# A float32 product replaced by three float32r passes in a one-core local-attention stack

## The chip, the cores and the metric

One core of one Trainium2 chip runs the whole kernel as a single program. The metric is device time in microseconds (us). TensorE (PE) multiplies; VectorE (DVE), ScalarE (ACT) and GpSimd (POOL) work on vectors; SyncE (SP) issues the DMAs.

## The reference, cut to what matters

Tokens: 1 x 2048 x 128, float32. A six-layer stack runs twice, with the same weights, and between the two runs stands a linear-attention block with a feed-forward part of its own. Each layer of the stack is:

```
x = attn_layer(shift_tokens(x)) + x     # 16 heads of 64, windows of 32 tokens, l2-normed q and k
x = ffn_layer(shift_tokens(x)) + x
def ffn_layer(x, g, bln, W1, b1, W2, b2):
    xn = (x - mu) / sqrt(var + 1e-05) * g + bln
    hg = xn @ W1 + b1                   # W1: 128 x 682
    a, gate = split(hg, 2)              # 341 each
    return a * gelu(gate) @ W2 + b2
```

The change is in `xn @ W1` and in the buffer that holds `a * gelu(gate)`.

## The kernel before, in words

**Tiling.** Activations lie transposed, 128 features on the partitions. The attention works on chunks of 128 tokens, 16 a layer (`CH`), the feed-forward on groups of 512 tokens, 4 a layer (`NG`). `stack(inv)` is written once for each engine and called twice. It is a software pipeline: each engine runs a loop over `t` (about 108 steps), and in step `t` does its share of chunk `t`, `t - 1`, `t - 2` and so on. Step `t` of PE overlaps step `t` of ACT and of DVE and step `t + 1` of POOL.

**The feed-forward in four phases.** `phase(n)` gives `(n - LAG) % 4` and the group. In phase 0 PE centres the group (L528) and makes the variances (L560); in phase 1 POOL makes the diagonals (L1290), PE spreads them (L531), DVE multiplies (L1029, `XN`), ACT adds the bias in place (L811, `xn_done`). In phases 2 and 3 PE makes the wide layer: `hidden` (L513 to L519) multiplies 114, 114 and 113 columns of `W1` with `XN` (128 x 512), float32; phase 2 makes the gate (ACT's gelu into `GB`, L815), phase 3 the other half (DVE's product into `HT`, L1036). In phase 1 of the next group PE multiplies `HT` with `W2` (L545, `y_done`). One product of each phase stands in `ffn_first`, ahead of the transposes of keys and queries (L340, `turn_keys`, `turn_queries`); two stand at the end of PE's step (`ffn_second`, `ffn_third`), ahead of the next step's scores (L450, L439). 48 groups, 2 phases, 3 products: 288 products. A float32 product is two records in the profile.

**The attention's projection.** `project` (L388 to L390) already multiplies in three passes, of a high and a low part each of the activation (`XH`, `XL`) and of the weights (`WH`, `WL`), all float32r. The weights' parts are made one layer ahead, in thirds `k` = 0, 1, 2: SP loads a third into `WSTAGE` (L1387), ACT rounds it in phase 1 (L804), POOL subtracts in phase 2 (L1299, `w_split`). Third 0 is split in phase 2 of the last group of the layer before, third 1 in that of the layer's first group, third 2 in that of its second.

**GpSimd's step**, in order: sines of the queries (L1240), low part of `x` (L1217, L1220), `add_keys` (L1282), `add_queries` (L1266), `ffn` (L1290 in phase 1, L1299 in phase 2), `scale_queries` (L1275, waits for the norms that DVE makes at L918), the table (L1234), sines of the keys (L1240, wait for PE's transposes). `turn_queries` on PE waits for L1275.

**SyncE's step** (L1376 to L1399) for chunk `c`: `window_values` waits for ACT's copy of the values (L770, `v_kept`) and issues 16 DMAs (L1373, L1374); then a rotary table (L1336). In steps 1, 5 and 9 of a layer it waits for `w_split` (L1386) before it loads the next third, in step 7 for the products of the layer before (`hid`) before it loads `W1`, in step 9 for `y_done` before it loads `W2`. ACT's copy L770 of chunk `c` waits for the window DMAs of chunk `c - 1` (L767), and PE's projection of the next keys (L388) waits for L770.

Of the kernel before, what the change touches and what calls it, by code (L numbers as in the profile page):

```python
# [7 lines left out]
F32 = mybir.dt.float32  # L8
F32R = mybir.dt.float32r
BF16 = mybir.dt.bfloat16  # L10
I32 = mybir.dt.int32
ALU = mybir.AluOpType
ACT = mybir.ActivationFunctionType
AX = mybir.AxisListType

P = 128
NTOK = 2048
CH = 16
GT = 512
NG = NTOK // GT  # L20
DEPTH = 6
HEADS = 16
# [4 lines left out]
DI = 341  # L27
# [10 lines left out]
NGR = DEPTH * NG  # L38

S_G, S_B, S_B2, S_B1A, S_B1G, NSMALL = 0, 1, 2, 3, 6, 9  # L40
# [54 lines left out]
def build(nc, a, out):  # L95
    ctx = ExitStack()
    with ctx:  # L97
        def sb(name, shape, dt=F32):
            return ctx.enter_context(nc.sbuf_tensor(name, shape, dt))

        def sem(name):
            return ctx.enter_context(nc.semaphore(name))
# [19 lines left out]
        WO = sb("WO", [P, 2, NP_, P])  # L122
        QKS = sb("QKS", [P, 2, 4 * DH])
        W1 = sb("W1", [P, 2 * DI])
        W2 = sb("W2", [P, 3, P])
        SMALL = sb("SMALL", [P, 2, NSMALL])

# [1 line left out]
        XL = sb("XL", [P, 2, P], F32R)  # L129
        RAWQK = sb("RAWQK", [P, 2, HEADS, DH])  # L130
        SQ = sb("SQ", [P, 2, HEADS, DH])
        SSM = sb("SSM", [P, HEADS])
        RN = sb("RN", [P, 2, HEADS + 4])
        NY = sb("NY", [P, NORMS])
        NV = sb("NV", [P, NORMS])
# [3 lines left out]
        QT = sb("QT", [P, NP_, P])  # L139
        KT = sb("KT", [P, NP_, WIN + P])  # L140
        MX = sb("MX", [P, 2, NP_])
        SUM = sb("SUM", [P, 2, HEADS])
        PR = sb("PR", [P, HEADS, 2 * WIN])
        PT = sb("PT", [P, NP_, P])
# [7 lines left out]
        DIAG = D2  # L152
        DG = sb("DG", [P, GT])
        XN = sb("XN", [P, GT])
        GB = sb("GB", [P, 3, GT])
        HT = sb("HT", [P, 3, GT])

        def flat(x):
            return x.rearrange("p a b c -> p (a b c)")
# [27 lines left out]
        PS = ctx.enter_context(nc.psum_tensor("PS", [P, 8, 512], F32))  # L187
# [19 lines left out]
        weighed = [sem("weighed%d" % r) for r in range(2)]; o_scaled = sem("o_scaled"); o_rows = sem("o_rows"); o_kept = sem("o_kept")  # L207
        projected = sem("projected"); xb_done = sem("xb_done"); xa_done = sem("xa_done")
        xf_done = sem("xf_done"); centred = sem("centred"); d2_done = sem("d2_done"); dg_done = sem("dg_done"); var_done = sem("var_done"); var_kept = sem("var_kept")
        diag_done = sem("diag_done"); spread = sem("spread"); z_done = sem("z_done"); xn_done = sem("xn_done")  # L210
        hid = [sem("hid%d" % i) for i in range(3)]; gelu_done = sem("gelu_done"); ht_done = sem("ht_done"); y_done = sem("y_done")
        m_cen = sem("m_cen"); m_d2 = sem("m_d2"); m_dg = sem("m_dg"); m_var = sem("m_var"); m_r = sem("m_r")
        m_diag = sem("m_diag"); m_rb = sem("m_rb"); m_ln = sem("m_ln")
# [9 lines left out]
        A_DMAS, F1_DMAS, F2_DMAS, V2_DMAS = 3, 1, 2, 16  # L223
# [22 lines left out]
        def group_count(inv, g):  # L246

            return inv * NGR + g + 1
# [39 lines left out]
        def _(pe):  # L288
# [55 lines left out]
            def stack(inv):  # L344
# [168 lines left out]
                def hidden(g, t, bank):  # L513
                    at, n = FT[t % 3]
                    at += 0 if t >= 3 else DI
                    if g % NG == 0:
                        pe.wait_ge(f1_w, 16 * F1_DMAS * (inv * DEPTH + g // NG + 1))
                    pe.wait_ge(xn_done, group_count(inv, g))
                    pe.matmul(PS[0:n, bank, :], W1[:, at:at + n], XN[:, :], start=True, stop=True).then_inc(hid[t % 3], 1)  # L519

                def ffn_first(n):
                    q, g = phase(n)
# [14 lines left out]
                def ffn_second(n):  # L537
                    q, g = phase(n)
                    if q == 1 and 0 <= g - 1 < NGR:
# [4 lines left out]
                        for i, (_, m) in enumerate(FT):  # L544
                            mm = pe.matmul(PS[:, B_F2, :], W2[0:m, i, :], HT[0:m, i, :], start=(i == 0), stop=(i == 2))  # L545
                        mm.then_inc(y_done, 1)
# [75 lines left out]
            for g in range(NG):  # L622
                q = group(QB, g)
# [17 lines left out]
            for g in range(NG):  # L641
                for n in range(4):
                    if g > 0:
                        pe.wait_ge(mg_ready, 4 * g - 3 + n)
                    pe.matmul(PS[:, 3 + n, :], FC1[:, n * P:(n + 1) * P], XNM[:, g, :], start=True,
                              stop=True).then_inc(mh_ready, 1)
# [15 lines left out]
        def _(act):  # L662
# [12 lines left out]
            def stack(inv):  # L675
# [116 lines left out]
                def ffn_late(n):  # L792
                    q, g = phase(n)
                    if q == 3 and 0 <= g + 1 < NGR:
                        act.wait_ge(xb_done, count(inv, 4 * (g + 1) + 3))
                        at = (g + 1) % NG * GT
                        held(centred, group_count(inv, g))
                        act.activation(XF[0:DH, :], XB[0:DH, at + 1:at + 1 + GT], ACT.Copy)
                        act.activation(XF[DH:P, :], XB[DH:P, at:at + GT], ACT.Copy).then_inc(xf_done, 1)
                    if q == 1 and 0 <= n < NCH and n % CH >= 4:  # L800
                        k, w = (n % CH) // 4 - 1, layer_of(inv, n) + 1
                        if w < 2 * DEPTH:
                            act.wait_ge(w_in, 16 * (3 * w + k - 2))
                            act.activation(WH[:, w % 2, k * HEADS * DH:(k + 1) * HEADS * DH], WIN_[:, :],  # L804
                                           ACT.Copy).then_inc(w_high, 1)
                    if not 0 <= g < NGR:
                        return
                    s = (inv * DEPTH + g // NG) % 2
                    if q == 1:
                        act.wait_ge(z_done, group_count(inv, g))  # L810
                        act.activation(XN[:, :], XN[:, :], ACT.Identity, bias=SMALL[:, s, S_B:S_B + 1]).then_inc(xn_done, 1)  # L811
                    elif q == 2:
                        for i, (_, m) in enumerate(FT):
                            act.wait_ge(hid[i], 2 * (inv * NGR + g) + 1)
                            act.activation(GB[0:m, i, :], PS[0:m, (B_F1, B_F2, B_F3)[i], :], ACT.Gelu,  # L815
                                           bias=SMALL[0:m, s, S_B1G + i:S_B1G + i + 1]).then_inc(gelu_done, 1)

# [36 lines left out]
            for g in range(NG):  # L854
                a = 2 * (g % 2)
# [10 lines left out]
            for g in range(NG):  # L866
                for n in range(4):
                    act.wait_ge(mh_ready, 4 * g + n + 1)
                    if g >= 2:
                        act.wait_ge(my_ready, g - 1)  # L870
                    act.activation(HTM[g % 2][:, n, :], PS[:, 3 + n, :], ACT.Gelu,
                                   bias=MSMALL[:, M_FC1B + n:M_FC1B + n + 1]).then_inc(mg_ready, 1)
# [10 lines left out]
        def _(dve):  # L883
# [37 lines left out]
            def stack(inv):  # L921
# [54 lines left out]
                def row_max(c):  # L976
# [4 lines left out]
                    s = rows(B_S).rearrange("p b (j k) -> p b j k", k=2 * WIN)  # L981
                    dve.tensor_reduce(MX[:, :, :], s, AX.X, ALU.max)  # L982
                    dve.drain()
# [69 lines left out]
            def norm_all(b, o, bias=None, done=None, at=(5, 6)):  # L1053
                dve.wait_ge(m_var, 4 * b + 4)
                dve.tensor_copy(SSM[:, :], PS[:, VAR, 0:16])
                dve.drain()
                r = RN[:, 0, 0:HEADS]
                rsqrt([(r, slice(0, HEADS))], SSM[:, :], NY[:, 0:HEADS], NU[:, 0:HEADS], NV[:, 0:HEADS], EPS, ALU.add).then_inc(m_r, 1)
                dve.drain()
# [24 lines left out]
            def norm_twice(b, first, second, gain, bias):  # L1084
                dve.wait_ge(m_var, 4 * b + 4)
                dve.tensor_copy(SSM[:, :], PS[:, VAR, 0:16])
                dve.tensor_copy(SUM[:, 0, :], PS[:, VAR, 0:16])
                dve.drain()
                r, rr = RN[:, 0, 0:HEADS], RN[:, 1, 0:HEADS]
                rsqrt([(r, slice(0, HEADS))], SSM[:, :], NY[:, 0:HEADS], NU[:, 0:HEADS], NV[:, 0:HEADS], EPS, ALU.add).then_inc(m_r, 1)  # L1090
                dve.drain()
                dve.scalar_tensor_tensor(SSM[:, :], SUM[:, 0, :], RSQRT_UNIT * RSQRT_UNIT, r, ALU.mult, ALU.mult)
                dve.drain()
                dve.tensor_tensor(SSM[:, :], SSM[:, :], r, ALU.mult)
                dve.drain()
# [100 lines left out]
        def _(pool):  # L1196
            def held(signal, value):

                if value > 0:
                    pool.wait_ge(signal, value)  # L1200
# [8 lines left out]
            def stack(inv):  # L1209
# [74 lines left out]
                def ffn(n):  # L1284
                    q, g = phase(n)
                    if q == 1 and 0 <= g < NGR:
                        c = n - 1 + CHAIN_OFF
                        pool.wait_ge(norms, chain_count(inv, c))
                        for j in range(4):
                            ins = pool.tensor_scalar(DIAG[:, j * P:(j + 1) * P], EYE[:, :],  # L1290
                                                     RN[:, c % 2, HEADS + j:HEADS + j + 1], None, ALU.mult)
                        ins.then_inc(diag_done, 1)
                    m = n - 1
                    if q == 2 and 0 <= m < NCH and m % CH >= 4:
                        k, w = (m % CH) // 4 - 1, layer_of(inv, m) + 1
                        if w < 2 * DEPTH:
                            pool.wait_ge(w_high, 3 * w + k + 1)
                            cols = slice(k * HEADS * DH, (k + 1) * HEADS * DH)
                            pool.tensor_tensor(WL[:, w % 2, cols], WIN_[:, :], WH[:, w % 2, cols].bitcast(F32),  # L1299
                                               ALU.subtract).then_inc(w_split, 1)  # L1300
# [16 lines left out]
        def _(sp):  # L1317
# [26 lines left out]
            def load_w1(w):  # L1344
                l = w % DEPTH
                sp.dma_start(W1[:, :], a["w1"][l:l + 1].rearrange("l p n -> p (l n)")).then_inc(f1_w, 16)

            def load_w2(w):
                l = w % DEPTH
                sp.dma_start(W2[0:FT[0][1], 0:2, :],  # L1350
                             a["w2"][l:l + 1, 0:FT[2][0]].rearrange("l (i p) n -> p (l i) n", i=2)).then_inc(f2_w, 16)
                sp.dma_start(W2[0:FT[2][1], 2, :], a["w2"][l:l + 1, FT[2][0]:DI].rearrange("l p n -> p (l n)")).then_inc(f2_w, 16)

# [109 lines left out]
```

## Time and profile before

| | us |
|---|---|
| median of 3 runs | 3620.34 (3605.24 to 3626.68) |
| the profiled execution, its own time | 3621.26 |
| its span, first to last instruction | 3619.1 |
| PE busy | 3322.5 (92%) |
| DVE busy | 2800.4 (77%) |
| POOL busy | 2720.1 (75%) |
| ACT busy | 2482.6 (69%) |
| mean granted TensorE clock | 0.969 of 2.4 GHz |

The two stacks take nearly all of the span, from about 35 to 1756 us and from about 1910 us to the end. Matmuls overlap in the array, so the distance from the start of one matmul to the start of the next says what it costs PE, and the length of its record does not.

### The profile page before, as it was taken

The numbers are of one execution on the slowest core, as the hardware profiler recorded it, in microseconds if no ns is written. First come the engines' busy times: TensorE is split into PE (matmuls) and PEld (weight loads), VectorE is DVE, ScalarE is ACT, GpSimd is POOL, SyncE is SP. The second block draws the span as 40 slices with busy tenths as digits, with TensorE's granted clock in tenths as the row PEclk, the third lists the DMA queues.
The fourth block names the chain that finished last, engine by engine and source line by source line (L and its number), as shares of the span: only waits on it lengthen the run. The fifth ranks groups of instructions, "written<-read, shape, count | busy, mean of one in ns | idle before, by whom it ended". The sixth has DMA issues, their size and how long they took to land. (4 is left out here: it accounts for less than half of the span.)

```text
span 3619.1 us, 152088 instructions
## 1 busy us (share of the span) xinstructions
PE 3322.5 (92%) x64040; PEld 2535.6 (70%) x64040; DVE 2800.4 (77%) x4983; ACT 2482.6 (69%) x3080; POOL 2720.1 (75%) x2152
## 2 busy tenths in 40 slices
PE   6899999999999999998677899999999999999996
PEld 4777777777777777776335777777777777777774
DVE  5778878788878878876447788778888878878883
ACT  4677777777767777775225677777777777777773
POOL 5888888788878878875007888888888888888881
PEclk8999999999999999999889999999999999999998
DMA  3333333333333333332002333333333333333320
GB/s 96 77 83 82 80 83 82 78 86 79 79 84 78 80 87 77 81 88 64 6 0 67 79 85 82 80 84 78 83 86 78 81 83 80 81 83 77 78 74 25
DMA packets 208997, 272.66 MB, mean 75 GB/s; under 512 B 55748, under 2 KB 103744, under 8 KB 208320
## 3 DMA queue, kind: packets, MB, share of 16 engines
q1 hardware_dynamic: 208320, 262.94, 28.2%
q8 instruction: 510, 8.36, 1.0%
q14 instruction: 167, 1.37, 0.1%
HBM read 60.35 MB, written 1.05 MB: 17 GB/s over the span
## 5 line engine op out<-in xcount | busy, mean ns | idle before, releaser
L1240 POOL TENSOR_TENSOR V<-RAWQK,TAB 128x512 f32<-128x512 f32 x768 | 953.2, 1275 | 443.5 <-PE PS L340 434.3
L388 PE MATMUL PS<-WH,XH 128*128 128x512 f32 x1152 | 518.4, 450 | 99.9 <-ACT VS L770 86.3
L770 ACT ACTIVATE VS<-PS 128x1024 f32<-128x1024 f32 x192 | 196.5, 1023 | 481.0 <-PE PS L390 357.2
L1282 POOL TENSOR_TENSOR V<-V,U 128x1024 f32<-128x1024 f32 x192 | 455.6, 2373 | 14.9
L390 PE MATMUL PS<-WL,XH 128*128 128x512 f32 x1152 | 465.5, 404 | 0.0
L389 PE MATMUL PS<-WH,XL 128*128 128x512 f32 x1152 | 464.5, 403 | 0.0
L1266 POOL TENSOR_TENSOR V<-V,U 128x1024 f32<-128x1024 f32 x192 | 457.5, 2383 | 0.0
L1275 POOL TENSOR_TENSOR V<-V,RN 128x1024 f32<-128x1024 f32 x192 | 372.2, 1938 | 93.7 <-DVE RN L918 92.1
L340 PEld LDWEIGHTS PS<-EYE,V 128*128 128x128 f32 x3072 | 348.2, 141 | 110.2 <-issue 99.0
L510 PEld LDWEIGHTS PS<-OT,WO 128*128 128x128 f32 x3072 | 373.6, 192 | 21.4 <-issue 5.1
L340 PE MATMUL PS<-EYE,V 128*128 128x128 f32 x3072 | 371.3, 274 | 10.3 <-ACT OT L777 5.1
L510 PE MATMUL PS<-OT,WO 128*128 128x128 f32 x3072 | 375.8, 276 | 3.3 <-DVE XN L1029 3.1
L439 PEld LDWEIGHTS PS<-KT,QT 64*32 64x32 f32 x24576 | 263.1, 105 | 126.4 <-issue 125.2
L940 DVE TENSOR_TENSOR U<-PS,TAB 128x1024 f32<-128x1024 f32 x192 | 234.3, 1220 | 139.9 <-issue 110.0
L439 PE MATMUL PS<-KT,QT 64*32 64x64 f32 x24576 | 303.0, 225 | 37.7 <-issue 37.1
L474 PE MATMUL PS<-V,PT 64*32 64x64 f32 x24576 | 336.4, 224 | 0.8 <-issue 0.4
L388 PEld LDWEIGHTS PS<-WH,XH 128*128 128x128 f32 x1152 | 223.5, 194 | 154.3 <-issue 98.0
L982 DVE TENSOR_REDUCE MX<-PS 128x16 f32<-128x1024 f32 x192 | 234.3, 1220 | 113.0 <-PE PS L439 112.0
L474 PEld LDWEIGHTS PS<-V,PT 64*32 64x32 f32 x24576 | 273.0, 105 | 68.1 <-issue 64.5
L519 PE MATMUL PS<-XN,W 128*114 128x512 f32 (+1 forms) x576 | 297.9, 630 | 5.3 <-ACT XN L811 4.6
L1002 DVE TENSOR_TENSOR ON<-PS,SUM 128x1024 f32<-128x1024 f32 x192 | 235.1, 1225 | 82.7 <-PE PS L474 75.3
L699 ACT ACTIVATE RAWQK<-PS 128x1024 f32<-128x1024 f32 x192 | 196.7, 1025 | 117.2 <-PE PS L390 117.2
(162 smaller groups left out, 7100.0 us busy)
## 6 DMA issues: line engine op xcount, KB each, us to landing
V<-VS SPq DMA_DIRECT2D x3072, 64.0 KB
ROTB<-c_rot SPq DMA_DIRECT2D x192, 128.0 KB, 2.5
WSTAGE<-wqkv SPq DMA_DIRECT2D x33, 512.0 KB
WO<-wo SPq DMA_DIRECT2D x12, 512.0 KB, 3.8
W<-w SPq DMA_DIRECT2D x12, 341.0 KB, 3.1
QKS<-qks SPq DMA_DIRECT2D x12, 128.0 KB, 3.7
W<-w SPq DMA_DIRECT2D x12, 114.0 KB
RAWQK<-x SPq DMA_DIRECT2D x4, 256.0 KB, 3.7
```

The costliest lines, as they stand in the source:

```text
L340: mm = pe.matmul(PS[:, bank + h // 4, (h % 4) * P:(h % 4 + 1) * P], src(h), EYE[:, :], is_transpose=True, start=True, stop=True, skip_grou ...
L388: pe.matmul(o, XH[:, p, :], WH[:, w, cols], start=True, stop=False)
L389: pe.matmul(o, XL[:, p, :], WH[:, w, cols], start=False, stop=False)
L390: mm = pe.matmul(o, XH[:, p, :], WL[:, w, cols], start=False, stop=True)
L439: mm = pe.matmul(PS[WIN * w:WIN * (w + 1), B_S + r, j * 2 * WIN:(j + 1) * 2 * WIN], QT[DH * r:DH * (r + 1), j, WIN * w:WIN * (w + 1)], KT[ ...
L474: mm = pe.matmul(PS[WIN * w:WIN * (w + 1), B_O + r, j * DH:(j + 1) * DH], PT[DH * r:DH * (r + 1), j, WIN * w:WIN * (w + 1)], V2[DH * r:DH ...
L510: mm = pe.matmul(PS[:, B_WO, 0:P], WO[:, w % 2, h, :], OT[:, h, :], start=(h == 0), stop=(h == NP_ - 1))
L519: pe.matmul(PS[0:n, bank, :], W1[:, at:at + n], XN[:, :], start=True, stop=True).then_inc(hid[t % 3], 1)
L1240: ins = pool.tensor_tensor(paired(V[:, k])[:, :, :, h * half:(h + 1) * half], split(RAWQK[:, k])[:, :, :, (1 - h) * half:(2 - h) * half], ...
L1266: pool.tensor_tensor(V[:, 0], V[:, 0], U[:, 0], ALU.add).then_inc(q_turned, 1)
L1275: pool.tensor_tensor(v, v, rn, ALU.mult).then_inc(q_scaled, 1)
L1282: pool.tensor_tensor(V[:, 1], V[:, 1], U[:, 1], ALU.add).then_inc(k_turned, 1)
```

## The change

`W1` is split once a layer, and `XN` once a group, into float32r high and low parts; `hidden` makes three passes. ACT writes `XNH` before it writes `XN`, and rounds `W1` after it when the group is its layer's first. POOL makes `W1L` (in the first group) and `XNL` in its phase-2 slot, ahead of L1299. PE waits for `xn_low` and `w1_low`. `HT` becomes another name of `GB`, and the gelu waits for the product with `W2` of the group before. `SSM` becomes another name of `MX`.

```diff
+        W1H = sb("W1H", [P, 2 * DI], F32R)
+        W1L = sb("W1L", [P, 2 * DI], F32R)
...
-        SSM = sb("SSM", [P, HEADS])
...
+        SSM = MX[:, :, :].rearrange("p a b -> p (a b)")
...
+        XNH = sb("XNH", [P, GT], F32R)
+        XNL = sb("XNL", [P, GT], F32R)
         GB = sb("GB", [P, 3, GT])
-        HT = sb("HT", [P, 3, GT])
+        HT = GB
...
                     if g % NG == 0:
-                        pe.wait_ge(f1_w, 16 * F1_DMAS * (inv * DEPTH + g // NG + 1))
-                    pe.wait_ge(xn_done, group_count(inv, g))
-                    pe.matmul(PS[0:n, bank, :], W1[:, at:at + n], XN[:, :], start=True, stop=True).then_inc(hid[t % 3], 1)
+                        pe.wait_ge(w1_low, inv * DEPTH + g // NG + 1)
+                    pe.wait_ge(xn_low, group_count(inv, g))
+                    pe.matmul(PS[0:n, bank, :], W1H[:, at:at + n], XNH[:, :], start=True, stop=False)
+                    pe.matmul(PS[0:n, bank, :], W1H[:, at:at + n], XNL[:, :], start=False, stop=False)
+                    pe.matmul(PS[0:n, bank, :], W1L[:, at:at + n], XNH[:, :], start=False, stop=True).then_inc(hid[t % 3], 1)
...
                         act.wait_ge(z_done, group_count(inv, g))
+                        act.activation(XNH[:, :], XN[:, :], ACT.Identity, bias=SMALL[:, s, S_B:S_B + 1])
                         act.activation(XN[:, :], XN[:, :], ACT.Identity, bias=SMALL[:, s, S_B:S_B + 1]).then_inc(xn_done, 1)
+                        if g % NG == 0:
+                            act.wait_ge(f1_w, 16 * F1_DMAS * (inv * DEPTH + g // NG + 1))
+                            act.activation(W1H[:, :], W1[:, :], ACT.Copy).then_inc(w1_high, 1)
                     elif q == 2:
                         for i, (_, m) in enumerate(FT):
                             act.wait_ge(hid[i], 2 * (inv * NGR + g) + 1)
+                            held(y_done, group_count(inv, g - 1))
...
+                    if q == 2 and 0 <= g < NGR:
+                        if g % NG == 0:
+                            pool.wait_ge(w1_high, inv * DEPTH + g // NG + 1)
+                            pool.tensor_tensor(W1L[:, :], W1[:, :], W1H[:, :].bitcast(F32), ALU.subtract).then_inc(w1_low, 1)
+                        pool.wait_ge(xn_done, group_count(inv, g))
+                        pool.tensor_tensor(XNL[:, :], XN[:, :], XNH[:, :].bitcast(F32), ALU.subtract).then_inc(xn_low, 1)
                     m = n - 1
                     if q == 2 and 0 <= m < NCH and m % CH >= 4:
                         k, w = (m % CH) // 4 - 1, layer_of(inv, m) + 1
```

## Rows read from the trace of the kernel before

**Rows 1.** The page: busy us, share of the span, instructions.

```profile
PE 3322.5 (92%) x64040; PEld 2535.6 (70%) x64040; DVE 2800.4 (77%) x4983; ACT 2482.6 (69%) x3080; POOL 2720.1 (75%) x2152
```

**Rows 2.** Window: length, busy of PE, PEld, DVE, ACT, POOL; PEclk, DMA, GB/s.

```profile
789.00:960.00 171.00, 167.56 (x3428) 130.72 (x3434) 145.78 (x252) 129.75 (x161) 141.47 (x114) 1.00 0.32 82
```

**Rows 3.** Waits: engine, line, releaser; us in total, times, longest.

```profile
SPq L1387 <- POOL WL L1299: 197.1, 22, 10.2
...
ACT VS L770 <- issue: 123.8, 25, 8.8
...
PE PS L388 <- ACT VS L770: 86.3, 30, 5.6
```

**Rows 4.** Timelines of POOL, SP, ACT, PE around the second stall of a layer.

```profile
739.61 4.97 POOL L1240 TENSOR_TENSOR V<-RAWQK,TAB 128x512 f32<-128x512 f32 x4 [2.09 <-PE PS L340]
...
765.85 2.40 POOL L1299 TENSOR_TENSOR WL<-WSTAGE,WH 128x1024 fp32r<-128x1024 f32 x1
...
768.27 0.33 SPq L1387 DMA_DIRECT2D WSTAGE<-wqkv  x1
...
784.03 1.02 ACT L770 ACTIVATE VS<-PS 128x1024 f32<-128x1024 f32 x1 [5.69 <-issue]
...
785.20 0.77 PE L388 MATMUL PS<-WH,XH 128*128 128x512 f32 x1 [4.17 <-ACT VS L770]
```

**Rows 5.** The same around the first stall of that layer.

```profile
693.27 2.39 POOL L1299 TENSOR_TENSOR WL<-WSTAGE,WH 128x1024 fp32r<-128x1024 f32 x1
...
710.82 1.02 ACT L770 ACTIVATE VS<-PS 128x1024 f32<-128x1024 f32 x1 [4.84 <-issue]
...
711.99 0.47 PE L388 MATMUL PS<-WH,XH 128*128 128x512 f32 x1 [3.54 <-ACT VS L770]
```

**Rows 6.** PE's timeline: six float32r matmuls, then one and two float32 products.

```profile
604.71 0.50 PE L388 MATMUL PS<-WH,XH 128*128 128x512 f32 x1
605.05 0.40 PE L389 MATMUL PS<-WH,XL 128*128 128x512 f32 x1
...
606.21 1.95 PE L510 MATMUL PS<-OT,WO 128*128 128x128 f32 x16
...
630.62 1.11 PE L519 MATMUL PS<-XN,W 128*114 128x512 f32 x2
631.57 1.91 PE L340 MATMUL PS<-EYE,V 128*128 128x128 f32 x16
...
634.20 1.97 PE L519 MATMUL PS<-XN,W 128*114 128x512 f32 x4
636.00 0.59 PE L450 MATMUL PS<-MASK,EYEB 128*128 128x512 bf16 x2
```

**Rows 7.** Groups by line on POOL and ACT: busy us, mean ns.

```profile
L1234 POOL TENSOR_TENSOR TAB<-ROTB,QKS 128x256 f32<-128x256 f32 x192 | 140.9, 734 | 0.2
...
L1299 POOL TENSOR_TENSOR WL<-WSTAGE,WH 128x1024 fp32r<-128x1024 f32 x33 | 79.1, 2398 | 0.0
...
L811 ACT ACTIVATE XN<-XN,SMALL 128x512 f32<-128x512 f32 x48 | 34.7, 723 | 117.1 <-DVE XN L1029 117.1
```

**Rows 8.** POOL's timeline in phase 2, without and with L1299 in the slot.

```profile
628.05 1.94 POOL L1275 TENSOR_TENSOR V<-V,RN 128x1024 f32<-128x1024 f32 x1 [1.39 <-DVE RN L918]
...
699.57 4.96 POOL L1240 TENSOR_TENSOR V<-RAWQK,TAB 128x512 f32<-128x512 f32 x4 [1.32 <-PE PS L340]
```

**Rows 9.** ACT's timeline in phase 1: the bias, then the values' copy.

```profile
621.50 0.72 ACT L811 ACTIVATE XN<-XN,SMALL 128x512 f32<-128x512 f32 x1 [2.46 <-DVE XN L1029]
...
623.56 1.02 ACT L770 ACTIVATE VS<-PS 128x1024 f32<-128x1024 f32 x1 [1.34 <-PE PS L390]
```

**Rows 10.** Windows of 15 us that begin where PE restarts after a stall.

```profile
712.00:727.00 15.00, 14.22 (x180) 10.39 (x180) 8.06 (x9) 11.07 (x14) 5.08 (x5) 0.77 0.32 81
...
987.40:1002.40 15.00, 13.99 (x311) 10.19 (x312) 10.71 (x14) 12.00 (x15) 8.57 (x9) 1.00 0.40 105
```

**Rows 11.** PE's timeline at the end of the first stack: its last six products.

```profile
1744.00 7.07 PE L519 MATMUL PS<-XN,W 128*114 128x512 f32 x12 [2.28 <-ACT XN L811]
```

More of the change, by code:

```diff
@@ L209, in build @@
         xf_done = sem("xf_done"); centred = sem("centred"); d2_done = sem("d2_done"); dg_done = sem("dg_done"); var_done = sem("var_done"); var_kept = sem("var_kept")
-        diag_done = sem("diag_done"); spread = sem("spread"); z_done = sem("z_done"); xn_done = sem("xn_done")
+        diag_done = sem("diag_done"); spread = sem("spread"); z_done = sem("z_done"); xn_done = sem("xn_done"); xn_low = sem("xn_low"); w1_high = sem("w1_high"); w1_low = sem("w1_low")
         hid = [sem("hid%d" % i) for i in range(3)]; gelu_done = sem("gelu_done"); ht_done = sem("ht_done"); y_done = sem("y_done")
```

## The prediction

> **What bounds the kernel now.** I read the page first [rows 1]. PE is busy for 92% of the span, no other engine for 80%. The windows say more: between two stalls, in the 171 us from 789 to 960 us, PE is busy for 167.56 us at the full 2.4 GHz [rows 2]. PE is the bound there, and what is taken off PE's stream comes off the time.
>
> The waits then show an exception [rows 3]. 22 times SP waits for POOL's L1299, ACT's copy L770 waits 25 times for something that is no engine, and PE's L388 waits 86.3 us for that copy. The timelines explain it [rows 4]. POOL ends L1299 at 768.25, SP issues at 768.27 the load that waited for it, and behind that load stand the 16 window DMAs of a chunk. Those DMAs wait behind it: SP's wait lasts 10.2 us at the longest [rows 3]. L770 runs when they have landed, 15.8 us after L1299's end, and PE restarts 1.17 us later, after 4.17 us of idling. The first stall of the layer is the same chain: L1299 ends at 695.66, L770 starts at 710.82, PE idles 3.54 us [rows 5]. A stack's layer has two of them, behind thirds 0 and 1; the third has no SP step waiting for it in time. With 33 thirds split in this loop there are 11 first and 11 second stalls.
>
> Ahead of each L1299 POOL works without a break from the sines at the end of phase 0: 739.61 to 765.85 in the second case, with no idle row between [rows 4]. The chain is therefore: PE's transposes in phase 0, POOL for 26.2 us, L1299, SP, L770, PE. Between a stall's end and the next phase 0 it is PE's own stream. **Anything put into POOL's phase-2 slot ahead of L1299 lengthens this chain one for one, and what PE saves in that same phase is swallowed by the stall.**
>
> **PE's saving.** Six float32r matmuls in a row take 606.21 - 604.71 = 1.50 us start to start [rows 6]: 0.34 for the first, 0.232 for each of the others. So one product of three passes costs 0.34 + 2 x 0.232 = 0.80 and a pair 1.50. The float32 product alone takes 631.57 - 630.62 = 0.95, the pair 636.00 - 634.20 = 1.80 [rows 6]. A phase saves 0.15 + 0.30 = 0.45 us, all 96 phases 43.2 us. Not all of it is on the path. Phase 2 lies between L1299 and the stall in 20 cases: 11 second stalls, and 9 first ones, as the first third of each stack's layer 0 is split before there is a group. That leaves 76 x 0.45 = **34.2 us gained**.
>
> A rule bears on this size. A float32 matmul is two records here, at 0.45 to 0.475 us each [rows 6]. The Trainium skill, "FP8 and Floating Point Precision", section "TensorE Precision Notes", gives true float32 four passes of high and low parts; three of four would save a quarter, 0.24 + 0.45 = 0.69 a phase, which would make the gain an estimated 52 us. The rows' 0.34 for a first pass speaks against so much.
>
> **POOL's part.** No row has these subtractions. 256 columns take 734 ns and 1024 take 2398 ns [rows 7], so 2.17 ns a column and 0.18 us of start: 512 columns (`XNL`) 1.29 us, 682 columns (`W1L`) 1.66 us. Bounds: two 256-column ones, 1.47, and half a 1024-column one, 1.20; I take the line between, as dtype and form are L1299's own. 9 first stalls move by 1.29 = 11.6 us, 11 second ones by 1.29 + 1.66 = 2.95: 32.5 us. Together **44.1 us lost**.
>
> In other groups the slot is covered. Without L1299, `XNL` falls into POOL's 1.39 us of waiting for DVE's norms [rows 8]. With it (third 2), POOL waits 1.32 us for PE after the slot [rows 8], and XNL fits in with 0.03 to spare. If this cover were gone, 26 groups would lose up to 1.29 us each, 34 us (the second rival). What is queued behind the slot is L1275 and the table, and PE's `turn_queries` waits for L1275. In the step of [rows 6, 8] the slot opens at 628.05 - 1.39 = 626.66, and the queries are turned in the second half of L340 x16, from 632.5. With L1299 (2.35), `XNL` (1.29) and L1275 (1.94) it would be 632.2: just in time. With `W1L` as well, 633.9: 1.4 us late, but that is a second stall's step, and the wait disappears in the stall. PE's new wait for `xn_low` ends at 626.66 + 1.29 = 627.95, or with `W1L` at 629.6, ahead of the product at 630.62 [rows 6]. `xn_done` is there in time: XN ends at 622.22 [rows 9], and `XNH` adds 0.7.
>
> **ACT's part.** `XNH` is one more L811, 0.72 us [rows 7], before a copy L770 that waits 1.34 us for PE [rows 9]: covered. In 12 groups `W1H` comes on top; between 0.72 (512 columns, L811) and 1.06 (1024 columns, L804) I take 0.8. The sum, 1.5, exceeds the cover by 0.2 us; I take 0, and at the most 12 x 0.4 = 5 us if PE's keys wait for it. The gelu's new wait and `HT` over `GB` cost 0: the product that it waits for stands a whole step of PE ahead of the gate's own products, for which the gelu waits anyway. `SSM` is used only outside the loops. No DMA is added or moved in the program; SP's waits for `hid` end a little sooner.
>
> **The stacks' ends.** There the last group's chain lies bare: PE's products wait for ACT [rows 11]. `XNH` 0.7 and `XNL` 1.3 with their two handovers delay it by 2.0, the group before by about 0.3: 2 x 2.3 = **4.6 us lost**. Their saving is in the 76 phases.
>
> **The clock.** A first stall now ends either without a fall of the clock (granted 1.00) or with one (0.77, at times down to 1.2 GHz) [rows 10]; the difference is 0.23 x 15 = 3.4 us at the most, and nothing at the least, where PE would have waited for exponentials anyway. Of the 9 that grow, 5 restart at 1.00. They grow by 1.29 + 0.45 = 1.74 us of idling, second stalls by 3.4. I take 1.5 us for five first stalls and 0.2 for each second: **10 us lost**, between 0 and 17 + 11 x 1 = 28.
>
> **Sum.** -34.2 + 44.1 + 4.6 + 10 = +24.5 us on the profiled execution's 3621.3 (span 3619.1, 2.2 around it), so 3645.8. That execution is 0.9 us over the median: I predict 3645. A measurement of this kernel can tell about 0.5%, 18 us, from no change (three runs lay 21 us apart).
>
> **Rivals.**
> (a) *PE is the bound and the slot is covered* (faster, 0.15). The chain through SP would have slack of 3 us that I don't see. For it: PE's 98% in [rows 2] and SP's other waits. Against: L770's waits are for no engine, and SP issues 0.02 us after L1299 ends [rows 4]. Then 43.2 - 4.6 = 38.6 come off: 3582.
> (b) *The slot costs in all groups* (slower by more, 0.10). POOL becomes the bound once its phase 2 takes over 1.32 us more with L1299, or 1.39 without [rows 8]; that decides at a price of `XNL` just above mine. 48 x 1.29 + 12 x 1.66 = 82 on the path against 43.2, plus 4.6 and 10: +53, 3674.
> (c) *The passes run denser* (no change, 0.27). If a first pass costs 0.232 as well, a phase saves (0.95 - 0.70) + (1.80 - 1.39) = 0.66, and 76 phases 50.2 us; with 44.1 + 4.6 lost and a clock term of 5: +4, 3624. The page of the Trainium skill named above leads to the same case.
> (d) *The three passes cost what two records do* (slower, 0.05). If W1H's reload between passes were not hidden, the gain falls to zero: 44 + 5 + 10 = +59, 3679. Against: L389 reloads the array too and keeps 0.232 us.
>
> **How the numbers follow.** My forecast gets 0.43, of which 0.04 ends within 18 us of no change, where the clock term is near 0. Slower is 0.39 + 0.10 + 0.05 = 0.54, same 0.27 + 0.04 = 0.31, faster 0.15. With terms of both signs this size, the range reaches from 3600 (half of (a)'s gain, and all of (c)) to 3670 (the clock's upper bound, 18 us over my value, and a POOL price of 1.47 for `XNL`: 20 x 0.18 = 4); the forecast's own range is 3628 to 3670.
>
> **What would show it.** L519's records should be replaced by three kinds with starts 0.23 apart and a first one at 0.34. L1299 should start 1.3 us later after its L1266 with thirds 0 and 2, 2.95 us with third 1. L770 should stay 15 to 17 us behind L1299's end. PE's wait L388 for L770 should grow from 86.3 by about 20 x 0.45 + 44 = 53 us, to some 140, and ACT's wait for no engine from 123.8 to about 170. PE's busy time should fall by some 30 us. The window between two stalls should shorten by 5 x 0.45 = 2.2 us. The prediction is wrong if L770's waits for no engine don't grow (then (a)), if `turn_queries` waits for L1275 in groups without a stall (then (b)), or if an alone-standing product takes 0.7 us (then (c)).

## The result and the profile after

The changed kernel takes 3642.8 us in the median of 11 runs, beside 3619.5 of the kernel before; the ratio is 1.0067, with a 95% interval from 1.0051 to 1.0083. It is slower by 24 us (18 to 30). One of the 11, at 4064.3 us and a mean clock of 0.74, fell in a slow state and is left out of the ratio. The profiled execution has a span of 3640.3 us and a mean clock of 0.963.

The page of the changed kernel, its busy times, beside [rows 1]:

```profile
PE 3297.3 (91%) x64328; PEld 2586.5 (71%) x64328; DVE 2800.9 (77%) x4983; ACT 2525.9 (69%) x3140; POOL 2800.8 (77%) x2212
```

PE is busy for 25 us less and POOL for 81 us more, and yet the kernel is slower. The waits, beside [rows 3], say where it went (engine, line, releaser; us in total, times, longest; L1404 is the old L1387, L776 the old L770, L392 the old L388):

```profile
SPq L1404 <- POOL WL L1316: 243.8, 22, 13.0
ACT VS L776 <- issue: 152.1, 26, 8.5
PE PS L392 <- ACT VS L776: 116.8, 35, 6.6
...
POOL V L1286 <- DVE RN L929: 57.5, 79, 2.9
...
PE PS L344 <- POOL V L1286: 14.4, 12, 2.0
```

SP waits 47 us longer for POOL's split, PE 30 us longer for ACT's copy, and PE's transposes wait 12 times for POOL's L1286, 14.4 us in all, beside 0.4 us for the old L1275 before. Ten of the 12 stand in the steps that have `W1L`, `XNL` and a third in POOL's slot, 1.1 to 2.0 us each. The groups by line of POOL and ACT, with the new instructions (busy us, mean ns):

```profile
L1309 POOL TENSOR_TENSOR XNL<-XN,XNH 128x512 fp32r<-128x512 f32 x48 | 61.5, 1282 | 35.0 <-ACT XN L818 35.0
...
L817 ACT ACTIVATE XNH<-XN,SMALL 128x512 fp32r<-128x512 f32 x48 | 34.7, 722 | 117.7 <-DVE XN L1040 117.7
...
L1307 POOL TENSOR_TENSOR W1L<-W,W1H 128x682 fp32r<-128x682 f32 x12 | 19.9, 1655 | 0.0
...
L821 ACT ACTIVATE W1H<-W 128x682 fp32r<-128x682 f32 x12 | 9.1, 757 | 0.0
```

And the timelines around the same second stall as in [rows 4]: POOL's slot, SP's load, ACT's copy, PE's two waits.

```profile
749.25 4.96 POOL L1251 TENSOR_TENSOR V<-RAWQK,TAB 128x512 f32<-128x512 f32 x4
...
757.57 2.38 POOL L1277 TENSOR_TENSOR V<-V,U 128x1024 f32<-128x1024 f32 x1
759.91 1.64 POOL L1307 TENSOR_TENSOR W1L<-W,W1H 128x682 fp32r<-128x682 f32 x1
761.52 1.28 POOL L1309 TENSOR_TENSOR XNL<-XN,XNH 128x512 fp32r<-128x512 f32 x1
762.76 2.39 POOL L1316 TENSOR_TENSOR WL<-WSTAGE,WH 128x1024 fp32r<-128x1024 f32 x1
765.10 1.94 POOL L1286 TENSOR_TENSOR V<-V,RN 128x1024 f32<-128x1024 f32 x1
...
765.18 0.33 SPq L1404 DMA_DIRECT2D WSTAGE<-wqkv  x1
...
781.31 1.02 ACT L776 ACTIVATE VS<-PS 128x1024 f32<-128x1024 f32 x1 [7.44 <-issue]
...
767.10 1.09 PE L344 MATMUL PS<-EYE,V 128*128 128x128 f32 x8 [1.34 <-POOL V L1286]
...
782.48 0.76 PE L392 MATMUL PS<-WH,XH 128*128 128x512 f32 x1 [6.43 <-ACT VS L776]
```

The third's split starts 762.76 - 759.91 = 2.85 us after the slot opens, where before it opened the slot. From its end (762.76 + 2.39 = 765.15) to ACT's copy it is 16.2 us, much as before (15.8). PE then idles 6.43 us where it idled 4.17.

PE's timeline in phase 2, beside [rows 6]: one product, the transposes, then the pair.

```profile
627.78 0.49 PE L523 MATMUL PS<-XNH,W1H 128*114 128x512 f32 x1
628.11 0.40 PE L524 MATMUL PS<-XNL,W1H 128*114 128x512 f32 x1
628.34 0.39 PE L525 MATMUL PS<-XNH,W1L 128*114 128x512 f32 x1
628.57 1.91 PE L344 MATMUL PS<-EYE,V 128*128 128x128 f32 x16
...
631.20 0.49 PE L523 MATMUL PS<-XNH,W1H 128*114 128x512 f32 x1
...
632.70 0.61 PE L454 MATMUL PS<-MASK,EYEB 128*128 128x512 bf16 x2
```

The single product costs 628.57 - 627.78 = 0.79 us and the pair 632.70 - 631.20 = 1.50, for 0.95 and 1.80.

### The profile page after: what moved, and what is told of

Read it like the earlier page. It is cut to its first block, busy times and chain, and to the rows that moved or that the text cites. A ratio compares the mean times of both kernels' runs of the same rounds, so it can differ in the third digit from the quotient of the medians.

```text
span 3640.3 us, 152925 instructions
## 1 busy us (share of the span) xinstructions
PE 3297.3 (91%) x64328; PEld 2586.5 (71%) x64328; DVE 2800.9 (77%) x4983; ACT 2525.9 (69%) x3140; POOL 2800.8 (77%) x2212
## 4 chain that ended last, share of the span: by engine, by line
PE 73%; POOL 10%; issue 9%; ACT 4%; DVE 3%; DVEq 1%; POOLq 0%; SPq 0%; DMA 0%; ACTq 0%
PE PS L344 17%; PE PS L392 7%; PE PS L478 7%; PE PS L443 7%; PE PS L394 6%; PE PS L393 6%; PE PS L514 5%; POOL V L1251 3%; PE PS L551 3%; PE PS L523 3%; PE PS L454 2%; PE PS L524 2%; PE PS L525 2%; POOL V L1293 2%; POOL V L1277 1%
## 5 line engine op out<-in xcount | busy, mean ns | idle before, releaser
L392 PE MATMUL PS<-WH,XH 128*128 128x512 f32 x1152 | 523.4, 454 | 128.0 <-ACT VS L776 116.8
L776 ACT ACTIVATE VS<-PS 128x1024 f32<-128x1024 f32 x192 | 196.9, 1026 | 461.3 <-PE PS L394 308.2
L1286 POOL TENSOR_TENSOR V<-V,RN 128x1024 f32<-128x1024 f32 x192 | 372.1, 1938 | 62.4 <-DVE RN L929 57.5
L344 PE MATMUL PS<-EYE,V 128*128 128x128 f32 x3072 | 373.9, 274 | 24.4 <-POOL V L1286 14.4
L392 PEld LDWEIGHTS PS<-WH,XH 128*128 128x128 f32 x1152 | 225.0, 195 | 185.1 <-issue 131.3
L394 PEld LDWEIGHTS PS<-WL,XH 128*128 128x128 f32 x1152 | 224.1, 195 | 56.3 <-issue 0.6
```

What stands on the lines that cost most here:

```text
L344: mm = pe.matmul(PS[:, bank + h // 4, (h % 4) * P:(h % 4 + 1) * P], src(h), EYE[:, :], is_transpose=True, start=True, stop=True, skip_grou ...
L392: pe.matmul(o, XH[:, p, :], WH[:, w, cols], start=True, stop=False)
L394: mm = pe.matmul(o, XH[:, p, :], WL[:, w, cols], start=False, stop=True)
L1286: pool.tensor_tensor(v, v, rn, ALU.mult).then_inc(q_scaled, 1)
```

## The experiments

Every ratio is to the kernel before, in runs on the same chip; differences in us are differences of the ratios on 3620 us. The kernel before takes 3618 to 3626 us in the median on the three chips of these runs, so runs are compared by their ratios and not by their times. Lines of the changed kernel are meant unless the kernel before is named.

### Is it the wait in SP's step? (the kernel before, loads one step later)

```diff
-                    if i in (1, 5, 9) and w + 1 < 2 * DEPTH:
+                    if i in (2, 6, 10) and w + 1 < 2 * DEPTH:
```

> The kernel before, with SyncE's three loads of the next layer's thirds moved by one step (steps 2, 6 and 10 instead of 1, 5 and 9), so that the third before is already split when SyncE comes to its wait. If the chain L1299, SP, L770, PE is what stalls PE, the 22 stalls (about 79 us of PE idling at L388) and the clock's falls behind them (1 to 2 us each) go: about 3620 - 79 - 30 = 3510, between 3490 and 3545, and ACT's wait for no engine at L770 falls from 124 to under 30 us. Rival (a), in which that chain has slack, gives 3620. A third view, that the stalls are due to the 16 engines being busy with the third's 512 KB and not to the wait ahead of it, gives 3600 to 3620, since the load stays in front of a chunk's window DMAs.

Measured: 3509.4 us, ratio 0.9675 (0.9656 to 0.9694). One step later the split is done when SP comes to it, the waits are gone, and 118 us with them. The idling at the 22 stalls was 79 us of it; PE is also busy for 34 us less with the same instructions (3288.2 for 3322.5), at a mean clock of 0.980 for 0.969. Two of PE's waits in this kernel; the second is the one of [rows 3]:

```profile
PE PS L439 <- issue: 42.0, 44, 2.4
...
PE PS L388 <- ACT VS L770: 8.6, 9, 2.6
```

PE waits 8.6 us for ACT's copy instead of 86.3. The chain is shown, and that it was the wait and not the 512 KB that follow it: the load is still there, in front of a chunk's window DMAs.

### The changed kernel, loads one step later

> The changed kernel with the same shift of SyncE's loads. Without stalls PE's saving counts in all 96 phases (43 us) and POOL's added work ahead of L1316 costs nothing through SyncE; what is left against it are the stacks' ends (4.6 us) and, in the 11 steps that have W1L, XNL and a third in one slot, the queries' turn 1.4 us late (15 us, no longer hidden in a stall). Theory: 43 - 5 - 15 = 23 us under e1_before_late, so about 3487 if that is 3510; at least 10 us under it. Rival (b), POOL's slot is paid in all groups: 82 us of POOL against 43, 35 to 45 us over e1_before_late.

Measured: 3504.4 us, ratio 0.9663 (0.9649 to 0.9677), 4 to 5 us under the one above on the same chip. The two intervals overlap, so this is no gain that can be told from none, and the size is not as expected: 23 us, at least 10. Rival (b), 35 to 45 us over, is out. I measured PE's stream step by step in both traces, from one group of mask matmuls (L450, L454) to the next, in 156 steps (both stacks, layers 2 to 6); all of them together are 12 us shorter. The products take 178.1 us instead of 215.2, 37 us less, as priced. Given back: 13.5 us in the transposes of phase 2, all in the steps that have `W1L`, `XNL` and a third in POOL's slot, as expected; 6 net in the scores; the rest in pieces of 1 to 3 us. Two of PE's waits in this kernel:

```profile
PE PS L443 <- issue: 45.9, 59, 2.3
...
PE PS L344 <- POOL V L1286: 16.0, 12, 2.2
```

### The third's split first in POOL's slot

The two blocks of POOL's `ffn` change places, all else is as changed:

```diff
                     if q == 2 and 0 <= m < NCH and m % CH >= 4:
...
+                    if q == 2 and 0 <= g < NGR:
...
```

> The changed kernel, with the third's split (L1316) moved ahead of W1L and XNL in POOL's slot. All added work is still done. If its cost is its place ahead of the split, the 44 us and most of the clock's term come back: the stalls lie where they lay before, PE saves 34 us, the stacks' ends cost 5, so about 3592 (3585 to 3605), under the kernel before. XNL ends at 626.66 + 2.35 + 1.29 = 630.3 in the step looked at, against a product at 630.6, so PE should hardly wait for it. Rival: it is POOL's amount of work, not its place (b), or PE's three passes are no gain (d): then this stays at 3640 or goes higher, as xn_low comes 2.4 us later.

Measured: 3609.3 us, ratio 0.9948 (0.9928 to 0.9968): 19 us under the kernel before, 43 under the changed one (0.9948 - 1.0067 = -0.0119). So the 44 us lie in the place of the added work and not in its amount. The gain over the kernel before is 19 us where 28 were expected (3620 to 3592); the next run is short by as much. Three of its PE waits:

```profile
PE PS L392 <- ACT VS L776: 80.0, 28, 5.1
PE PS L443 <- issue: 52.2, 60, 2.6
...
PE PS L523 <- POOL XNL L1317: 26.0, 15, 4.2
```

The stalls are back at 80.0 us (86.3 before), and the products wait for XNL, 26.0 us in 15 cases against 9.9 in 4 in the changed kernel. The 16 us more lie in phase 2 of a layer's first group, 11 times, where W1L and the third stand ahead of XNL and a stall follows, which takes them up: PE idles there for 3.3 us in the mean, and for 4.5 before. What is missing shows in the scores, which take 13 us more than before in the 156 steps.

### The gain by itself

```diff
-                        pool.wait_ge(xn_done, group_count(inv, g))
-                        pool.tensor_tensor(XNL[:, :], XN[:, :], XNH[:, :].bitcast(F32), ALU.subtract).then_inc(xn_low, 1)
...
-                    pe.wait_ge(xn_low, group_count(inv, g))
+                    pe.wait_ge(xn_done, group_count(inv, g))
...
-                    pe.matmul(PS[0:n, bank, :], W1H[:, at:at + n], XNL[:, :], start=False, stop=False)
+                    pe.matmul(PS[0:n, bank, :], W1H[:, at:at + n], XNH[:, :], start=False, stop=False)
```

(and the same for `W1L`. This kernel leaves the low parts out of the product: it adds the product of the high parts three times.)

> The changed kernel without its POOL part: W1L and XNL are not made, and the second and third pass read the high parts again, so the low parts are left out of the product. PE's passes and ACT's XNH and W1H are all there. This is the gain by itself, with the old stalls: 76 x 0.45 = 34 us less, ACT's XNH at the stacks' ends 1.4 more, the clock 0 to 5 more: about 3589 (3583 to 3598). Rival (c), denser passes: 50 us less, 3570. Rival (d): 3620 or over.

Measured: 3605.6 us, ratio 0.9943 (0.9922 to 0.9965): 21 us less, 13 to 28 by the interval, where 31 were expected. Denser passes (rival c) are out: 50 were asked. In the 156 steps the products save 37 us here too; the scores take 10 us more than before, and the stalls at the thirds are 11 us longer, where 20 x 0.45 = 9 were priced.

### The cost by itself

```diff
-                    pe.matmul(PS[0:n, bank, :], W1H[:, at:at + n], XNH[:, :], start=True, stop=False)
-                    pe.matmul(PS[0:n, bank, :], W1H[:, at:at + n], XNL[:, :], start=False, stop=False)
-                    pe.matmul(PS[0:n, bank, :], W1L[:, at:at + n], XNH[:, :], start=False, stop=True).then_inc(hid[t % 3], 1)
+                    pe.matmul(PS[0:n, bank, :], W1[:, at:at + n], XN[:, :], start=True, stop=True).then_inc(hid[t % 3], 1)
```

> The changed kernel with PE's products as they were before (one float32 matmul of W1 and XN each), but with all else: ACT makes XNH and W1H, POOL makes XNL and W1L, PE waits for them. The parts are computed and not used. This is the cost by itself: 9 x 1.28 + 11 x (1.28 + 1.66) = 44 us through the chain, 4.6 at the stacks' ends, 0 to 10 for the clock: 49 to 59 us over the kernel before, 3670 to 3683 beside 3624. If the gain is 20 us, as e4_gain_alone has it, and the two simply add up to the 23 us measured, it is 43 over, 3664. Rival (b), all of POOL's 82 us paid: 3705 and more.

Measured: 3670.7 us, ratio 1.0132 (1.0112 to 1.0151): 48 us more, 41 to 55. That is 44.1 + 4.6 = 48.7 with nothing for the clock, or up to 6 us by the interval. POOL's whole 82 us (rival b) are out.

### The aliases by themselves

```diff
-        HT = sb("HT", [P, 3, GT])
+        HT = GB
...
+                            held(y_done, group_count(inv, g - 1))
```

(and `SSM` over `MX`, in the kernel before.)

> The kernel before with the two aliases alone: HT over GB, with the gelu's wait for the product of the group before, and SSM over MX. The prediction priced both at nothing: 0, within 5 us of the kernel before. Rival: the in-place product or the gelu's wait costs, 144 products of 0.74 us on DVE: if each took 10% longer or moved the exponentials behind it, 10 us or more over.

Measured: 3621.7 us, ratio 0.9998 (0.9986 to 1.0009). They cost nothing.

### W1 split earlier

```diff
+                    if q == 0 and 0 <= g < NGR and g % NG == 0:
+                        pool.wait_ge(w1_high, inv * DEPTH + g // NG + 1)
+                        pool.tensor_tensor(W1L[:, :], W1[:, :], W1H[:, :].bitcast(F32), ALU.subtract).then_inc(w1_low, 1)
                     if q == 2 and 0 <= g < NGR:
-                        if g % NG == 0:
...
                         pool.wait_ge(xn_done, group_count(inv, g))
```

(ACT makes `W1H` in phase 3 of the group before.)

> The changed kernel with the split of W1 made earlier: ACT rounds it in phase 3 of the group before, POOL subtracts in the new layer's phase 0, where POOL then waits about 2 us for PE. Nothing is left out. The chain to a layer's second stall gets shorter by W1L's 1.66 us, 11 times: 18 us under the changed kernel, and 2 to 5 more for the clock, so about 3622 beside 3643; the second stalls' PE idling falls from 6.5 to about 4.9 us. Rival: POOL's work costs by its amount and not by its place, then it stays within 3 us of the changed kernel.

Measured: 3625.5 us, ratio 1.0006 (0.9993 to 1.0019), 22 us under the changed kernel (1.0006 - 1.0067; 15 to 30). An instruction of 1.66 us, moved by two POOL steps, 11 times: 18 us by itself. The second stalls were expected to fall from 6.5 to 4.9 us, and they stay at 5.9 in the mean of the eleven; PE's wait hardly shrinks,

```profile
PE PS L392 <- ACT VS L776: 113.3, 34, 6.9
```

but the wait for L1286 is gone, so the two together fall from 116.8 + 14.4 = 131.2 us to 113.3, by 18. The chain shrinks by 2 us where `W1L` takes 1.66: from ACT's copy behind third 0 to the start of the next split it is 56.0 us in the mean of the eleven cases of the changed kernel, 54.0 here and 53.2 before.

### Both repairs together

The edit of the run before, with SP's line as well; nothing is left out of the product.

```diff
-                    if i in (1, 5, 9) and w + 1 < 2 * DEPTH:
+                    if i in (2, 6, 10) and w + 1 < 2 * DEPTH:
```

> e7_w1_early with SyncE's loads one step later as in e2_after_late. In e2_after_late PE's turn of keys and queries in a layer's third step of the first group is 1.35 us longer than in e1_before_late, 10 times in the 156 steps looked at; without W1L in that slot this should go: 12 to 15 us under e2_after_late's 3504, so 3490 (3485 to 3497), the fastest of all. If it stays at 3500 or over, what eats PE's saving is something else (the gaps in the scores in which PE waits for no engine).

Measured: 3490.6 us, ratio 0.9631 (0.9612 to 0.9650). This beats the kernel before by 3.7% and the late loads alone by 0.0044, 16 us (6 to 26). Under the changed kernel with late loads it is by 0.0032, 12 us, as expected of `W1L`'s new place. The page of this kernel:

```profile
PE 3250.9 (93%) x64328; PEld 2550.2 (73%) x64328; DVE 2800.7 (80%) x4983; ACT 2520.6 (72%) x3140; POOL 2801.9 (80%) x2212
```

### The gain without stalls

The edit of the gain by itself, with SP's line as well; the low parts are left out of the product here too.

```diff
-                    if i in (1, 5, 9) and w + 1 < 2 * DEPTH:
+                    if i in (2, 6, 10) and w + 1 < 2 * DEPTH:
```

> e4_gain_alone with SyncE's loads one step later: PE's three passes and ACT's parts, no POOL part, no stalls behind the thirds. The low parts are left out of the product. Against e1_before_late: 96 phases by 0.45 save 43 us, ACT's XNH at the stacks' ends costs 1.4, and the gaps inside the scores, in which PE waits for no engine, take back 8 to 12 (52.8 us in 50 gaps in e1_before_late, 61.6 in 69 in e2_after_late): 30 to 34 under 3509, about 3478, and 5 to 15 under e8_all's 3491, by the stacks' ends and POOL's slot. If the gaps are chance, it is 41 under, 3468; if POOL's slot costs nothing in e8_all, it is 3489.

Measured: 3473.6 us, ratio 0.9600 (0.9578 to 0.9621): 0.0075, 27 us, under the late loads alone (17 to 37), where 30 to 34 were expected and 41 if the scores' gaps were chance. The kernel with both repairs, which has the POOL part as well, takes 0.0031 more, 11 us (0 to 22). The expectation let the scores take back 8 to 12 us. This trace does not bear that out: their surplus in the 156 steps is 38.3 us beside 39.3 with the late loads alone, and the two profiled executions lie 43 us apart (3471.1 and 3514.5 us, the latter 7 us over its kernel's median).

### Where the scores wait for no engine

128 more waits for a semaphore that has long come stand at the head of PE's program, first in the kernel before with late loads, then in the kernel with both repairs:

```diff
             pe.wait_ge(init, 6)
-            pe.wait_ge(cast, 1)
+            for _ in range(129):
+                pe.wait_ge(cast, 1)
```

> e1_before_late with 128 more waits for a semaphore that has long come, at the head of PE's program: they move all of PE's instructions by 128 places and change nothing else. In the traces so far each gap of over 0.15 us inside the scores ends 1.2 to 1.6 us after one of the instruction queue's 16384-byte transfers has ended. If PE waits there for its own instructions, the gaps move to other phases with the places where those transfers' blocks end: in e1_before_late 29 us of the scores' surplus lie in phase 1 and 5 in phases 0 and 3 each; this split should change by more than 5 us, and the time by up to 15 us either way plus 2 to 5 for the waits. If the gaps come from what PE is asked to do in that phase (the product with W2 before it), they stay in phase 1 with 27 to 31 us.

> The same 128 waits at the head of PE's program of e8_all. In e8_all the surplus is 23 us in phase 1, 10 in phase 3, 7 in phase 0. By places in the instruction stream it should be split in another way, with a sum between 30 and 60 us, and the time within 15 us of 3491; by phases it stays as it is.

Measured: 3497.3 us, 0.9662 (0.9640 to 0.9684), beside 0.9675 without the waits; and 3483.6 us, 0.9626 (0.9600 to 0.9652), beside 0.9631. Neither time can be told from the kernel without the waits. 64 instructions were added, not 128. In the profiles the gaps in the scores, where two of their matmuls start over 0.15 us apart, are these:

| kernel | gaps | us | the scores' surplus over 1.94 us by phase 0, 1, 2, 3 |
|---|---|---|---|
| before | 52 | 48.9 | 5.4, 25.9, 0.0, 5.0 |
| after | 60 | 54.5 | 11.3, 20.1, 0.2, 8.8 |
| before, late loads | 50 | 52.8 | 5.5, 29.3, 0.1, 4.4 |
| the same, padded | 47 | 39.0 | 2.5, 22.5, 0.0, 1.9 |
| after, late loads | 69 | 61.6 | 12.1, 22.9, 0.4, 10.1 |
| both repairs | 63 | 55.5 | 7.2, 22.6, 0.4, 10.1 |
| the same, padded | 61 | 46.5 | 8.0, 19.5, 0.1, 10.4 |
| gain, late loads | 59 | 49.6 | 10.3, 17.8, 0.6, 9.6 |

(The surplus is counted over the 156 steps, from the first mask matmul to the first of the projection.) In every kernel each of these gaps ends 1.1 to 1.6 us after a transfer of 16384 bytes of queue q8, the instruction queue, has ended. The padding takes 7 us out of phase 1 in one kernel and 3 in the other, but most stays there, and no other phase gets more than 1 us in return. The first kernel's 22.5 us in phase 1 are outside the 27 to 31 that the rival named, and yet the gaps became fewer and did not move to other phases. So the gaps go with the instruction transfers in time, and more than that these two runs do not show. The traces of the other runs add one thing: of all thirteen traces, the five with float32 products have 47 to 52 such gaps (39 to 53 us), the eight with three passes 59 to 74 (46 to 69 us). Whether that comes from the number of instructions or from their places, these runs do not say.

## Why the prediction was right, point by point

**The time.** 3645 was predicted, 3642.8 measured, inside the forecast's own range, with the sign that had 0.54. The interval, 18 to 30 us, is clear of no change.

**The chain** was read rightly, and it is the heart of the case: the late loads take 118 us off the kernel before and nearly all of [rows 3]'s 86.3 us at L388. L770 starts 12.5 to 16.4 us behind the split's end at the 20 stalls of these two kinds, and 13.1 to 17.1 before: the 15 to 17 that were named come from two cases and are too narrow, the chain is the same. From PE's restart after a second stall to the next first stall, nine cases take 201.0 us in the mean before and 198.9 after; 2.2 less were forecast.

**POOL's part** held to a hundredth: XNL 1.282 us for 1.29, W1L 1.655 for 1.66, the line through [rows 7]. The lengthening by 2.95 us in front of a second stall shows as 53.2 to 56.0 us on the way from third 0's copy to the next split. Rival (a) fell with the result and the late loads, rival (b) with the cost by itself.

**PE's saving** was priced rightly per product (0.79 for 0.80, the pair 1.50) and passed on wrongly. The step that failed is "That leaves 76 x 0.45 = 34.2 us gained": it takes PE's stream to be free of other waits. Measured by itself, with ACT's 1.2 us at the stacks' ends, the gain is 21 us (13 to 28). The scores are the largest part that the traces show: 10 us more than before in the 156 steps of that run, 6 in those of the changed kernel with late loads. [rows 2] had room for such waits, 171 us with 167.56 busy, and I took the other 3.4 for nothing. The cause stays open in part: in the gain without stalls the scores take nothing back, and yet its medians show 27 us and not 41. Rivals (c) and (d) fell with the timeline of phase 2. The estimate from the Trainium skill, "FP8 and Floating Point Precision", section "TensorE Precision Notes" (three passes of four, 0.69 us a phase) does not agree: 0.16 + 0.30 = 0.46 us.

**The clock** was mis-sized: 10 us were put down, and the cost by itself leaves about nothing beside 48.7 us, in an interval of 41 to 55. What was to cause it came as forecast. The first stalls grew from 2.4 to 4.0 us in the mean of the nine, by 1.6 for 1.74; of the five with a granted clock of 1.00 in the 15 us behind them one still has it, and the others have 0.79 to 0.89; the mean clock of the run fell from 0.969 to 0.963. That PE runs slowly where it would wait anyway is argued and not shown; it fits that PE's wait for ACT's `PR` (L749, now L755) fell from 31.9 to 25.1 us.

**The two errors cancel.** The forecast was -34 + 59 = +25, the runs say -21 + 48 = +27, and the two together measure +24. The number is better than its terms.

**The second stalls** grew from 4.5 to 5.9 us in the mean of the eleven, not by the 3.4 forecast: 1.1 to 2.0 us of it stand in ten cases as PE's wait for L1286 in the step before, as the prediction had it ("1.4 us late"). The rest, some 0.7 us a case, may be saving of PE's that was gone before it arrived. That is also why PE's wait for L770 rose by 30 us to 116.8, not to some 140, and ACT's to 152 instead of 170.

**The stacks' ends** came as priced: PE's two waits for ACT and POOL there grew from 2.28 and 0.39 us to 4.24 and 0.69, in both stacks, 4.5 us for 4.6 (2.90 and 0.39 with ACT's part alone).

**ACT's part and the aliases.** The aliases by themselves cost nothing. ACT's part was not run by itself; PE's wait for L770 away from the 22 stalls went from 7.6 to 8.5 us, so at most about 1 us shows, within the 0 to 5 of the prediction.

## What to carry to other kernels

An engine with a quarter of its time free may still stand on the path in one slot: ask for each new instruction what is queued behind it on its engine, and who, on which queue, waits for that. Where, as here, the DMAs of one queue are issued in the program's order, a wait ahead of a load that nobody needs yet holds up all that is needed now; moving it by one step was worth 118 us, and the cheaper arithmetic 21 to 27. Put what is new behind what others wait for, or into a step in which the engine waits.

## What the runs showed of the hardware that I had not expected

PE's scores, 256 instructions in 1.41 us, break off 47 to 74 times a run in the thirteen traces, for 39 to 69 us in all, each time until 1.0 to 1.6 us after a 16384-byte transfer of the instruction queue has ended. That queue makes 510 such transfers in the kernel before, beside 2 x 64040 records of PE's matmuls and weight loads, about 251 records a transfer, and one block of scores is 256: by this estimate the scores use up about one transfer in 1.41 us. The kernel has more such waits with three float32r passes (59 to 74) than with float32 products (47 to 52), and 64 instructions without work at the program's head came with 9 and 14 us less of them in the profiled executions, though the medians could not tell the kernels apart. When a change adds or moves PE's instructions, this term is part of what it measures.
